# Six release blocks for the expert tiles where there were ten, with row tails cleared by plan and a new issue order

## Chip, core, metric

One core of a Trainium2 chip. The metric is the device time of one execution in microseconds; lower is better. The core's engines are PE (matrix multiply), DVE (vector), ACT (activation), POOL (here: indirect DMAs and small vector work) and SP (issues most DMAs).

## The reference, cut to what matters

```python
x = x + _L0_ffn(_L0_cond(x, dx, angle))        # bilinear warp of each 64x256 image, then a ternary-weight FFN (256-1024-256)
x = x + _L1_ffn(_L1_cond(x, ...))              # masked attention pooling, then 4 experts, each token goes to its top 2
x = x + _L2_ffn(_L2_cond(x, language_ids))     # adapter with layer norm, then a 256x256 frequency matrix
x = x + _L3_ffn(_L3_cond(x, cat_ids))          # per-image 256x256 matrix, then a ternary gate/up/down FFN
# in the experts:
h = gelu(einsum('nd,edh->enh', xf, w1) + b1)   # fp32, 256 -> 1024
y = einsum('enh,ehd->end', h, w2) + b2         # fp32, 1024 -> 256
out = einsum('nk,nkd->nd', gates, y_sel - c_sel + c_sum)   # of the two chosen experts
```

x has 128 images of 64 rows and 256 columns: 8192 tokens.

## The kernel before, in words

The images are worked in 32 groups of 4 (256 tokens, `QT`). Each engine runs a set of threads, written as Python generators: every `yield` ends a step, and `weave` (L214) strings the steps of all threads into one static instruction stream by a string of letters, `ORDER`, with one letter per step. Engines meet only at semaphores. So an engine that waits in one step holds up all that stands behind it in its string.

Per group there is a **front path**: POOL gathers windows of the image (`gather`, L1211), DVE does the warp (`warp`, L804 to L844), SP copies the result into row order (`regroup`, L624), then `front` (first FFN, L854 on DVE, L1489 on PE) and `attend` (pooling and router, L896, L1517). `attend` ends with a position for each of the 512 (token, expert) rows of the group; POOL writes the rows to their places in an arena in HBM (`scatter`, L1231), sorted by expert.

The groups are released to the experts in **blocks**, `BLOCKS` (L45): ten blocks of 2,2,3,4,4,4,4,4,3,2 groups. When the rows of a whole block are counted, `make_plan` (L982, DVE) writes which arena row and which expert each tile has. A block of n groups gets 2n full tiles of 256 rows and 3 half tiles of 128 (`NTILE`, `width`), since the four experts' shares do not end at tile borders. Per tile: SP loads its rows (L646) and 1 MB of the expert's first weights (L652), PE transposes (L1572), multiplies up (L1587) and down (L1603), ACT applies Gelu (L1389), DVE evicts (L1042), SP stores (L699). On PE the steps of two tiles overlap by one step.

When all tiles of a block are stored, `y_back` (POOL, L1245) gathers the rows of each of its groups back, and `back` (adapter and frequency matrix) and `last` (fourth layer, with the matmuls L1675, gate and up L1479, down L1485) finish the group. `back` and `last` have one set of buffers each and two of the image rows, so a group's `last` follows that of the group before.

The arena has two halves, used by blocks in turn. A tile may read rows that no token was written to, so the input arena is cleared first (L667), and the output arena too (L662): 17.8 MB of zeros from a row of zeros, at the head of SP's queue. The ternary weights of the two FFNs are made at the start from weights that SP loads one after another (L752); DVE's first reduction of each (L1162) waits for the load.

```python
NTILE = [2 * n * QT // TILE + EXP - 1 for n in BLOCKS]
pool.wait_ge(E["m_st"], 16 * TFIRST[BLOCK[q] + 1])    # y_back: all tiles of the block are stored
dve.wait_ge(E["run4"], BFIRST[b + 1])                 # make_plan: all groups of the block are counted
```

## Time and profile before

| | us |
|---|---|
| three runs | 2349.57, 2351.9, 2355.35; median 2351.9 |
| the profiled execution, span from first to last instruction | 2373.0 |
| first plan ready | 252.2 |
| first expert transposes on PE | 259.1 |
| last eviction of an expert tile ends | 2270.0 |

The profile's page gives busy times per engine and forty slices of the span, each digit a tenth of busy share. PEclk is the share of full clock that PE was granted. A row of the line groups ends with the idle time of the engine ahead of these instructions and what released it. Overlapping instructions of different lines are counted in each line's busy time, so the lines add up to more than the engine's own busy time.

### The profile page before, as it was taken

To read this page: it belongs to the slowest core of one execution; us is meant where nothing else is said; L and a number is where in the kernel's file an instruction comes from. 1 tells how busy PE (TensorE), PEld (TensorE's weight loads), DVE (VectorE), ACT (ScalarE), POOL (GpSimd) and SP (SyncE) were. 2 spreads that over 40 slices of the span, in tenths; PEclk is the share of its full clock that TensorE was granted. 3 is DMA by queue.
4 is the path that set the end of the run, shared out by engine and by line. 5 is a ranking of instruction groups with operands and counts; after the bars stand their busy time and mean duration, and the time that the engine had idled before them with its cause. 6 is when DMAs were issued, how large, how long until landed. Compare 5 with 4: busy or idle time off the path is not lost.

```text
span 2373.0 us, 47046 instructions
## 1 busy us (share of the span) xinstructions
PE 2056.5 (87%) x12000; PEld 1608.0 (68%) x12000; DVE 1769.0 (75%) x7891; ACT 1558.4 (66%) x2737; POOL 1029.2 (43%) x1092
## 2 busy tenths in 40 slices
PE   1065798999999999999999999999999999999965
PEld 1032577777777777777777777777777787778842
DVE  5589988878789888878988897789985454443444
ACT  1035566658686788768787878778875775765733
POOL 1356666645535564545446544456451212211120
PEclk8565799999999999999999999999999999999976
DMA  7833445454556455655556646456654555444521
GB/s 285 290 78 79 153 140 160 148 153 147 162 148 194 134 171 167 179 166 162 137 173 178 171 140 210 123 167 175 206 164 140 154 164 169 131 158 154 164 85 53
DMA packets 306118, 375.70 MB, mean 158 GB/s; under 512 B 127122, under 2 KB 251447, under 8 KB 292924
## 3 DMA queue, kind: packets, MB, share of 16 engines
q1 hardware_dynamic: 274848, 297.02, 41.7%
q0 software_dynamic: 28672, 68.21, 9.9%
q10 hardware_dynamic: 2332, 7.47, 0.8%
q8 instruction: 100, 1.64, 0.3%
q14 instruction: 166, 1.36, 0.2%
HBM read 291.23 MB, written 72.93 MB: 153 GB/s over the span
## 4 chain that ended last, share of the span: by engine, by line
PE 28%; DVE 11%; DMA 7%; SPq 7%; issue 5%; POOL 5%; ACT 1%; DVEq 1%; ACTq 0%; POOLq 0%
PE bank L1603 7%; PE bank L1587 7%; DMA w_win<-in_windows,w_idx 3%; PE bank L1479 3%; DVE w_prod L822 3%; POOL w_win L1211 2%; PE bank L1485 2%; PE bank L1657 2%; SPq L624 1%; PE bank L1467 1%; DMA moe_out_sorted<-moe_y 1%; DMA out<-x_back 1%; PE bank L1675 1%; DMA moe_y_back<-moe_out_sorted,rows_back 1%; PE bank L1473 1%
## 5 line engine op out<-in xcount | busy, mean ns | idle before, releaser
L1211 POOL DMA_INDIRECT w_win<-in_windows,w_idx x512 | 550.0, 1074 | 474.7 <-DMA w_win<-in_windows,w_idx 169.3
L1603 PE MATMUL bank<-moe_w,moe_hidden_T 128*128 x2528 | 634.4, 391 | 27.8 <-DVE moe_y L1042 19.2
L1587 PE MATMUL bank<-moe_xT,moe_w_tile 128*128 128x256 f32 (+1 forms) x3008 | 628.8, 353 | 4.0 <-ACT moe_xT L1372 3.9
L1587 PEld LDWEIGHTS bank<-moe_xT,moe_w_tile 128*128 128x128 f32 x3008 | 512.3, 194 | 74.9 <-issue 7.1
L1603 PEld LDWEIGHTS bank<-moe_w,moe_hidden_T 128*128 128x128 f32 x2528 | 469.8, 195 | 103.1 <-issue 42.6
L822 DVE TENSOR_TENSOR w_prod<-w_win,w_hat 128x36 f32<-128x36 f32 x4096 | 493.9, 216 | 6.8 <-issue 2.7
L1389 ACT ACTIVATE moe_hidden_T<-bank,moe_b 128x256 f32<-128x256 f32 (+1 forms) x752 | 288.4, 437 | 191.1 <-PE bank L1587 187.9
L1245 POOL DMA_INDIRECT moe_y_back<-moe_out_sorted,rows_back x128 | 127.7, 998 | 248.2 <-DVE rows_back L1052 116.4
L1231 POOL DMA_INDIRECT moe_in_sorted<-c,rows x128 | 139.2, 1088 | 150.4 <-issue 63.8
L1389 ACT ACT_TABLE_LOAD x128 | 164.2, 1283 | 56.2 <-PE bank L1587 54.6
L1129 DVE SCALAR_TENSOR_TENSOR hidden_back<-bank,back_stats,hidden_back 128x512 f32<-128x512 f32 x128 | 95.3, 744 | 110.8 <-ACT hidden_back L1429 110.2
L1429 ACT ACT_TABLE_LOAD x114 | 146.3, 1283 | 2.5
L879 DVE SCALAR_TENSOR_TENSOR hidden_front<-bank,front_stats,L_b_rows 128x512 f32<-128x512 f32 x128 | 95.2, 744 | 27.0 <-PE bank L1479 25.8
L1296 ACT ACTIVATE w_hat<-w_t 128x512 f32<-128x512 f32 x64 | 40.4, 631 | 113.4 <-DVE w_out L844 104.6
L1250 POOL TENSOR_SCALAR mean_var<-mean_var 128x2 f32<-128x2 f32 x32 | 14.3, 448 | 219.6 <-DVE mean_var L1082 219.0
L1429 ACT ACTIVATE hidden_back<-bank,back_stats 128x512 f32<-128x512 f32 x128 | 88.0, 688 | 31.6 <-PE bank L1479 30.1
L1479 PE MATMUL bank<-L_w_ternary,q1T_front 128*128 128x512 fp8e4 x256 | 84.4, 414 | 24.7 <-DVE hidden_front L879 21.9
L1042 DVE TENSOR_TENSOR moe_y<-bank,moe_offset_rows 128x512 f32<-128x512 f32 (+1 forms) x94 | 56.3, 599 | 63.0 <-PE bank L1603 38.0
L1479 PE MATMUL bank<-L_gate_ternary,q1T_back 128*128 128x512 fp8e4 x256 | 83.1, 409 | 23.2 <-DVE hidden_back L1129 20.9
L1359 ACT ACTIVATE q_front<-hidden_front,half_magic,front_tile_stats 128x1024 f16<-128x1024 f32 x64 | 79.3, 1239 | 28.5 <-DVE front_tile_stats L885 28.3
L1314 ACT ACTIVATE hidden_front<-hidden_front 128x1024 f32<-128x1024 f32 x64 | 67.7, 1058 | 44.4 <-DVE hidden_front L879 44.3
L1250 POOL TENSOR_SCALAR front_tile_stats<-front_tile_stats 128x1 f32<-128x1 f32 x64 | 16.8, 263 | 176.7 <-ACT q_front L1320 173.9
(258 smaller groups left out, 3803.0 us busy)
## 6 DMA issues: line engine op xcount, KB each, us to landing
moe_w_tile<-in_moe_w SPq DMA_DIRECT2D x94, 1024.0 KB
L_cond_W<-in_L_cond_W SPq DMA_DIRECT2D x128, 256.0 KB
adapters<-in_adapter SPq DMA_DIRECT2D x128, 192.5 KB
gamma_beta<-in_gamma_beta SPq DMA_DIRECT2D x128, 128.0 KB
moe_x<-moe_in_sorted SPq DMA_DIRECT2D x64, 256.0 KB
moe_out_sorted<-moe_y SPq DMA_DIRECT2D x64, 256.0 KB
x_front<-in_x SPq DMA_DIRECT2D x32, 256.0 KB
w_win<-in_windows,w_idx POOLq DMA_INDIRECT x512
```

Of the source, the lines that this page charges most:

```text
L822: ins = v.tensor_tensor(out3, win, hy, ALU.mult)
L879: v.scalar_tensor_tensor(HBA[:, n * 512:(n + 1) * 512], A0[:, :], sa[:, DQ][:, one(u)], b1B[:, n * 512:(n + 1) * 512], ALU.mult, ALU.add). ...
L1129: v.scalar_tensor_tensor(hb, B1[:, :], sbk[:, DQ][:, one(u)], hb, ALU.mult, ALU.mult).then_inc(E["b_hb"], 1)
L1211: gp.indirect_dma_start(out=V[:, g_ * WLEN:(g_ + 1) * WLEN], out_offset=None, in_=t["windows"], in_offset=bass.IndirectOffsetOnAxis(ap=idx ...
L1231: gp.indirect_dma_start(out=XS, out_offset=bass.IndirectOffsetOnAxis(ap=pos[par][:, c:c + 1], axis=0), in_=C1[:, u * D:(u + 1) * D], in_of ...
L1245: gp.indirect_dma_start(out=YG[:, c * D:(c + 1) * D], out_offset=None, in_=YS, in_offset=bass.IndirectOffsetOnAxis(ap=posb[:, c:c + 1], ax ...
L1359: return s.activation(to[:, :], hidden[:, :], ACT.Identity, bias=hmag[:, :], scale=scale)
L1389: ins = s.activation(hT[:, (f % (2 * FPU)) * TILE:(f % (2 * FPU)) * TILE + width(n)], (H0, H1)[r % 2][:, (f % FPU) * TILE:(f % FPU) * TILE ...
L1429: s.activation(HBB[:, n * 512:(n + 1) * 512], B0[:, :], ACT.Silu, scale=sbk[:, 6 * TT + u:6 * TT + u + 1]).then_inc(E["b_silu"], 1)
L1479: last = te.matmul(bank[:, :], q1t[:, d * QT + u * P:d * QT + (u + 1) * P], w[:, d * F + n * 512:d * F + (n + 1) * 512], start=(d == 0), s ...
L1587: last = te.matmul((H0, H1)[r % 2][:, (f % FPU) * TILE:(f % FPU) * TILE + width(n)], W1[n % 3][:, d * F + f * P:d * F + (f + 1) * P], XT[: ...
L1603: last = te.matmul(Y[:, u * D:(u + 1) * D], hT[:, (f % (2 * FPU)) * TILE + u * P:(f % (2 * FPU)) * TILE + (u + 1) * P], ap(moe2, weight + ...
```

## The change

`SUPERS` takes the place of `BLOCKS`: six blocks of 2, 4, 8, 8, 6 and 4 groups. `STRIDE` is 8, so no block is released in parts, and each has one plan of 2n + 3 tiles: 7, 11, 19, 19, 15 and 11, 82 where there were 94. The parts of `make_plan` for blocks released in several steps are in the code but never built.

Each expert's share of the arena gets 256 rows of slack. The input arena is no longer cleared at the start. When a block's plan is made, SP reads the four ends of the experts' rows from it and clears 256 rows behind each and 256 at the arena's end (`tails`); the block's first row load waits for these five writes. The output arena, larger now (18.9 MB in 20 writes), is cleared piece by piece behind the first groups (`zeros`), each piece after a given `a_x1`, the end of a group's front. Input and output arenas are two tensors each.

The four `ORDER` strings are new.

```diff
 TILE = 256
-BLOCKS = (2,2,3,4,4,4,4,4,3,2)
-NBK = len(BLOCKS)
-BFIRST = [sum(BLOCKS[:b]) for b in range(NBK + 1)]
-BLOCK = [b for b in range(NBK) for _ in range(BLOCKS[b])]
-NTILE = [2 * n * QT // TILE + EXP - 1 for n in BLOCKS]
+SUPERS = (2,4,8,8,6,4)
+STRIDE = 8
+HALVES = EXP - 1
+
+
+def steps():
+
+    out = []
+    for c, n in enumerate(SUPERS):
+        given = 0
+        for first in range(0, n, STRIDE):
+            groups = min(STRIDE, n - first)
+            final = first + groups == n
+            upto = 2 * n * QT // TILE + HALVES if final else 2 * (first + groups) * QT // TILE - (EXP - 1)
+            out.append((c, groups, upto - given, final))
+            given = upto
+    return out
...
+
+
+STEPS = steps()
+NSB, NBK = len(SUPERS), len(STEPS)
+SFIRST = [sum(SUPERS[:c]) for c in range(NSB + 1)]
+SUPER = [c for c in range(NSB) for _ in range(SUPERS[c])]
+BFIRST = [sum(g for _, g, _, _ in STEPS[:b]) for b in range(NBK + 1)]
+BLOCK = [b for b in range(NBK) for _ in range(STEPS[b][1])]
+NTILE = [n for _, _, n, _ in STEPS]
 TFIRST = [sum(NTILE[:b]) for b in range(NBK + 1)]
+STILE = [sum(n for k, _, n, _ in STEPS if k < c) for c in range(NSB + 1)]
 GT = TFIRST[NBK]
...
+def fresh():
+
+    out, seen = [], [0, 0]
+    for c, e in enumerate(ENDROW):
+        k = c % 2
+        new = [(c, k, r, min(ZSTEP, e + TILE - r)) for r in range(seen[k], e + TILE, ZSTEP)]
+        seen[k] = max(seen[k], e + TILE)
+        out += new
+    return out
+
+
+ZY = fresh()
+ZCOUNT = [sum(z[0] <= c for z in ZY) for c in range(NSB)]
 
 
...
 ORDER = {
     "vector":
-        "iciiciiiwiwiiwiwiwiwwiwiiwiwiwiwiwiwiwwwwiwiwiwiwwiwiwwiwiwiwiwiwwwwwwcwwwwifwfwfwiiffwiwifwfwwwfwffffwwfwwwfwwf"
...
+        "iiiciiiiiiwiwiwiwiwiiwwciwiwiwiwiiwwiiwiwiwiiwiwiwiwiwiwwwwwwwwwiwwwwiiwiwicfwffwfwwfwwfwfwwwfwffffwwfwwfwwfwfwf"
...
+                c, k, r, n = ZY[z]
+                sp.wait_ge(E["a_x1"], 2 * (max(SFIRST[c] - 2, 0) + (z - (ZCOUNT[c - 1] if c else 0)) // 3 + 1))
+                sp.dma_start(YS[k][r:r + n, :].rearrange("(p k) d -> p k d", p=P),
+                             ap(ZR, 0, [[0, n // P], [1, D]])).then_inc(E["z_y"], 16)
+
+            def tails(c):
+
+                yield
+                if c == 0:
+                    sp.wait_ge(E["z_set"], 1)
+                sp.wait_ge(E["plan"], BLOCK[SFIRST[c + 1] - 1] + 1)
+                if c > 1:
+                    sp.wait_ge(E["m_ld"], 16 * STILE[c - 1])
+                free = [sp.value_load(plan[0:1, PN_Z + EXP * c + e:PN_Z + EXP * c + e + 1], min_val=0, max_val=ENDROW[c])
+                        for e in range(EXP)]
+                for e in range(EXP):
+                    sp.dma_start(XS[c % 2][bass.ds(free[e], TILE), :].rearrange("(p k) d -> p k d", p=P),
+                                 ap(ZR, 0, [[0, TILE // P], [1, D]])).then_inc(E["zero"], 16)
+                end = ENDROW[c]
+                sp.dma_start(XS[c % 2][end:end + TILE, :].rearrange("(p k) d -> p k d", p=P),
+                             ap(ZR, 0, [[0, TILE // P], [1, D]])).then_inc(E["zero"], 16)
 
             def rows_in(n):
                 yield
...
                     for name in SCAT:
                         sp.wait_ge(E[name], 32 * BFIRST[TBLOCK[n] + 1])
+                    if STEPS[TBLOCK[n]][3]:
+                        sp.wait_ge(E["zero"], 16 * (EXP + 1) * (STEPS[TBLOCK[n]][0] + 1))
                 moe_rows(n)
...
                     yield
-                    if c == 0 and b < 4:
-                        pool.wait_ge(s_zero[b], 16 * len(pieces(ZX[b])))
                     if c == 0:
-                        if b > 1:
-                            pool.wait_ge(E["m_ld"], 16 * TFIRST[b - 1])
+                        if block > 1:
+                            pool.wait_ge(E["m_ld"], 16 * STILE[block - 1])
                         pool.wait_ge(E["a_pos"], q + 1)
                         pool.wait_ge(E["a_rc"], TT * (q + 1))
...
-                        pool.wait_ge(E["m_st"], 16 * TFIRST[BLOCK[q] + 1])
+                        pool.wait_ge(E["m_st"], 16 * STILE[SUPER[q] + 1])
```

Three places show how the strings move the work. First SP's queue at the start, where the zeros stand. Before:

```order
L667 DMA moe_in_sorted<-zero_row 1024x1x256 x2
L667 DMA moe_in_sorted<-zero_row 256x1x256
L667 DMA moe_in_sorted<-zero_row 1024x1x256 x2
L667 DMA moe_in_sorted<-zero_row 256x1x256
L662 DMA moe_out_sorted<-zero_row 1024x1x256 x4
L752 DMA raw<-in_L_gate 128x2048
L662 DMA moe_out_sorted<-zero_row 1024x1x256 x4
L662 DMA moe_out_sorted<-zero_row 512x1x256
L667 DMA moe_in_sorted<-zero_row 1024x1x256 x4
L752 DMA raw<-in_L_up 128x2048
```

With the change, at the same place:

```order
L630 DMA w_offsets<-w_offsets_all 1x128
L795 DMA raw<-in_L_gate 128x2048
L795 DMA raw<-in_L_up 128x2048
L620 DMA w_frac<-w_frac_all 128x2x16
L623 DMA w_shift_frac<-w_shift_frac_all 128x128 x2
L625 DMA w_idx<-w_idx_all 128x16
L795 DMA raw<-in_L_down 128x2048
L653 DMA c<-w_out 16x8x32 x12
```

The weight loads follow each other with no zeros between them; the zeros now stand among the regroup copies `c<-w_out`.

Second, PE at the border of two blocks. Before, ahead of the first tile of the third block:

```order
L1603 MATMUL bank<-moe_w,moe_hidden_T 128x256
L1473 MATMUL bank<-ident_f,q_front 128x128 x8
L1594 TENSOR_LOAD plan
L1603 ISA
L1603 MATMUL bank<-moe_w,moe_hidden_T 128x256
L1603 ISA
L1603 MATMUL bank<-moe_w,moe_hidden_T 128x256
L1572 MATMUL bank<-const,moe_x 128x128 x4
```

With the change, ahead of the first tile (L1637) of the third block, the first of eight groups:

```order
L1544 MATMUL bank<-L_gate_ternary,q1T_back 128x512 x2
L1544 MATMUL bank<-L_up_ternary,q1T_back 128x512 x2
L1626 MATMUL bank<-router_logits,const 128x8
L1627 MATMUL bank<-router_logits,ones 128x8
L1544 MATMUL bank<-L_gate_ternary,q1T_back 128x512 x2
L1544 MATMUL bank<-L_up_ternary,q1T_back 128x512 x2
L1544 MATMUL bank<-L_w_ternary,q1T_front 128x512 x2
L1538 MATMUL bank<-ident_f,q_front 128x128 x8
L1637 MATMUL bank<-const,moe_x 128x128 x4
```

Before, the first tile of each block from the second on follows the last tile of the block before at once. Now no expert matmul (L1652, L1668) stands in the 120 rows between the second block's last tile and this one; 3.7 groups' `front`, 3.9 `attend`, 3 `back` and 2.5 `last` do.

Third, PE behind the last expert matmul. Before:

```order
L1603 MATMUL bank<-moe_w,moe_hidden_T 128x256
L1473 MATMUL bank<-ident_f,q_back 128x128 x8
L1485 MATMUL bank<-L_down_ternary,q2T_back 128x256 x8
L1467 MATMUL bank<-const,x_back 128x128 x4
L1675 MATMUL bank<-L_cond_W,xT_last 64x256 x8
L1467 MATMUL bank<-ident_f,q_back 128x128 x4
```

With the change:

```order
L1668 MATMUL bank<-moe_w,moe_hidden_T 128x256
L1544 MATMUL bank<-L_gate_ternary,q1T_back 128x512 x2
L1544 MATMUL bank<-L_up_ternary,q1T_back 128x512 x2
L1532 MATMUL bank<-const,x_back 128x128 x4
L1544 MATMUL bank<-L_gate_ternary,q1T_back 128x512 x2
L1544 MATMUL bank<-L_up_ternary,q1T_back 128x512 x2
L1704 MATMUL bank<-xT_adapter,adapters 64x64 x8
```

Before, the group at work in `last` was group 28, at its down matmuls, and three L1675 (groups 29 to 31) were left. Now it is group 26, at its first gate matmul, and five of the same matmuls (L1740, groups 27 to 31) are left.

## Rows read from the trace of the kernel before

**Rows 1.** The page: span, busy times, two rows of the 40 slices.
```profile
span 2373.0 us, 47046 instructions
...
PE 2056.5 (87%) x12000; PEld 1608.0 (68%) x12000; DVE 1769.0 (75%) x7891; ACT 1558.4 (66%) x2737; POOL 1029.2 (43%) x1092
...
DVE  5589988878789888878988897789985454443444
...
GB/s 285 290 78 79 153 140 160 148 153 147 162 148 194 134 171 167 179 166 162 137 173 178 171 140 210 123 167 175 206 164 140 154 164 169 131 158 154 164 85 53
```

**Rows 2.** Table of stretches of the core, the columns named in its first line.
```profile
core 0: us, PE busy (x) PEld busy (x) DVE busy (x) ACT busy (x) POOL busy (x), PEclk, DMA share, GB/s
124.00:252.00 128.00, 73.51 (x278) 38.33 (x275) 114.26 (x622) 60.79 (x107) 82.48 (x82) 0.57 0.33 83
207.00:252.00 45.00, 26.57 (x90) 14.34 (x90) 39.34 (x223) 22.90 (x43) 32.47 (x33) 0.50 0.30 82
252.00:290.00 38.00, 30.92 (x151) 24.23 (x152) 35.65 (x199) 23.05 (x43) 20.52 (x25) 0.81 0.58 181
252.00:363.00 111.00, 100.26 (x529) 80.92 (x530) 101.16 (x547) 68.74 (x139) 63.93 (x71) 0.92 0.49 148
363.00:473.00 110.00, 99.71 (x560) 82.33 (x559) 95.67 (x533) 68.25 (x144) 74.67 (x74) 0.97 0.54 161
954.00:2270.00 1316.00, 1251.71 (x7525) 998.39 (x7523) 938.51 (x3962) 964.77 (x1644) 513.19 (x560) 0.97 0.54 162
2270.00:2373.00 103.00, 60.68 (x304) 33.63 (x304) 43.18 (x98) 31.18 (x44) 12.89 (x14) 0.67 0.26 78
```

**Rows 3.** Timeline of DVE, L844: start us, us, engine, line, operation, out<-in.
```profile
123.66 0.61 DVE L844 TENSOR_TENSOR w_out<-w_cols 128x256 f32<-128x256 f32 x1
...
241.73 0.61 DVE L844 TENSOR_TENSOR w_out<-w_cols 128x256 f32<-128x256 f32 x1
```

**Rows 4.** Groups by line and shape on PE: busy us, mean ns, idle before.
```profile
L1603 PE MATMUL bank<-moe_w,moe_hidden_T 128*128 x2528 | 634.4, 391 | 27.8 <-DVE moe_y L1042 19.2 <-ACT moe_hidden_T L1389 7.6 <-issue 0.3
L1587 PE MATMUL bank<-moe_xT,moe_w_tile 128*128 128x256 f32 x2048 | 496.1, 386 | 3.8 <-ACT moe_xT L1372 3.7
L1587 PE MATMUL bank<-moe_xT,moe_w_tile 128*128 128x128 f32 x960 | 132.8, 283 | 0.2 <-ACT moe_xT L1372 0.2
...
L1572 PE MATMUL bank<-const,moe_x 128*128 128x128 f32 x316 | 51.2, 278 | 1.5 <-DMA moe_x<-moe_in_sorted 1.5
```

**Rows 5.** Timeline of SP's queue near 60 to 90 us.
```profile
65.52 14.05 SPq L662 DMA_DIRECT2D moe_out_sorted<-zero_row  x5
...
89.62 2.62 SPq L752 DMA_DIRECT2D raw<-in_L_up  x1
```

**Rows 6.** Waits of DVE from 28 to 130 us: total us, times, longest.
```profile
DVE weight_sums L1162 <- DMA raw<-in_L_up: 15.3, 1, 15.3
DVE weight_sums L1162 <- DMA raw<-in_L_gate: 7.3, 1, 7.3
```

**Rows 7.** Timelines of DVE and PE around the first plan.
```profile
252.00 0.17 DVE L1026 TENSOR_TENSOR plan<-plan_work,const 128x21 int32<-128x21 f32 x1
...
259.11 1.06 PE L1572 MATMUL bank<-const,moe_x 128*128 128x128 f32 x4
```

**Rows 8.** The page, DMA issues: KB each, median us to landing.
```profile
moe_in_sorted<-zero_row SPq DMA_DIRECT2D x2, 256.0 KB, 7.7
```

**Rows 9.** The page, costliest groups: the eviction on DVE.
```profile
L1042 DVE TENSOR_TENSOR moe_y<-bank,moe_offset_rows 128x512 f32<-128x512 f32 (+1 forms) x94 | 56.3, 599 | 63.0 <-PE bank L1603 38.0
```

**Rows 10.** Timeline of PE behind the last expert tile.
```profile
2273.21 2.00 PE L1675 MATMUL bank<-L_cond_W,xT_last 128*64 128x256 f32 x16 [0.67 <-ACT xT_last L1417]
...
2279.19 1.03 PE L1479 MATMUL bank<-L_gate_ternary,q1T_back 128*128 128x512 fp8e4 x2 [0.69 <-ACT q1T_back L1363]
...
2309.38 2.00 PE L1675 MATMUL bank<-L_cond_W,xT_last 128*64 128x256 f32 x16 [0.68 <-ACT xT_last L1417]
...
2341.31 2.00 PE L1675 MATMUL bank<-L_cond_W,xT_last 128*64 128x256 f32 x16 [0.68 <-ACT xT_last L1417]
```

310 lines of the change are left out of this document (160 added, 150 removed).

## The prediction

> **What bounds the kernel now.** I read the page first. PE is busy 87% of the span and DVE 75%, but DVE's digits are high up to slice 30 and low behind it [rows 1]. The table of stretches then splits the run into three stages [rows 2]. From 954 to 2270 us PE works 1251.7 of 1316 us at a granted clock of 0.97: there PE sets the pace. From 124 to 252 us DVE works 114.3 of 128 us (89%) and PE 57%: there DVE does, through the warp. From 2270 us, the end of the last expert tile, to the end PE works 60.7 of 103 us and DVE 43.2: neither, but a chain of short steps through PE, ACT and DVE. The warps of the first and the fourth group end at 124.3 and 242.3 us [rows 3]: while DVE does little else, one group of the front path costs 39 us. So three things can move the end: the work on PE, the time at which PE is given tiles, and what is left when the tiles are done.
>
> **Sum, part by part.** The rows are of one execution of 2373.0 us span, 0.9% above the median of 2351.9; I add up in its time and scale by the ratio at the end.
>
> 1. *Fewer half tiles.* A block of n groups has 2n full and 3 half tiles: ten blocks give 64 and 30, six give 64 and 18. A half tile costs 132.8/30 = 4.4 us in L1587; L1603 did 2528 matmuls in 634.4 us, so its 16 take 4.0; two transposes 0.3: 8.8 us. A full one costs 496.1/64 = 7.8, 32 x 0.251 = 8.0 and 0.6: 16.4 us [rows 4]. Lines overlap: they add up to some 2336 us where PE is busy 2056.5, a factor of 0.88; and PE is busy 95% of the bound stretch. So 15.3 and 8.2 us of time. Twelve half tiles less are 98 us, if PE is the limit where they fall.
>
> 2. *The start.* Before, 17 MB of zeros stand on SP's queue ahead of two weight loads: from 65.5 us on nine of these writes are issued, and only at 89.6 us the load of the up weights [rows 5]. DVE waits 15.3 and 7.3 us for these loads [rows 6]. The new order issues both loads ahead of any zeros. Bounds 0 and 22.6 us; I take 18, since the wait is DVE's, and DVE bounds this stage. The first plan, ready at 252.2 us before [rows 7], now stands 4 us of DVE work later in its order: 238 us.
>
> 3. *Zeros later.* Twenty writes, eighteen of them of 1 MB, stand between the regroup copies of groups 1 to 15, seven of them in a row. Issue took 14.05 us for five [rows 5], so 2.8 each at most. A regroup copy behind seven could wait from 0 to 7 MB at the 285 GB/s of the first slice, 26 us [rows 1]; copies have a warp's time of slack, so I take 8. Here the shape of the queue matters. The Trainium skill, DMA: Bandwidth & Descriptors, section on queues, rings and completion order, says that SP has one row of rings whose descriptors are consumed in ring order; by that the copy waits for all seven and the sum would be 18 us higher. The load of the up weights, late behind zeros, agrees with it.
>
> 4. *The plan of the block of eight*, the third. This is the step on which most rests. DVE's work per group of the front path is 36 us (114.3 us [rows 2] for 3.2 warps, 3 fronts, 2.1 attentions). All of DVE is 1769.0 us [rows 1]: less 32 x 36, 56 us of evictions [rows 9] and 50 of preparation it leaves 16 us a group for back and last, 8 each. Up to the second plan DVE's order holds 4.1 groups of front path, 7 evictions and a plan: 155 us. Up to the third plan 7.9 groups (284 us), 5.0 backs and 3.9 lasts (70) and 11 evictions (10): 364 us. DVE's share in these stages is 0.89, 0.91 and 0.87, and 0.94 in the shortest stretch [rows 2]; I take 0.91. Second plan: 238 + 170 + 8 = 416 us. Third: 416 + 400 = 816. Before, groups came in blocks of 2, 2 and 3, each plan was in time, and PE was busy 91% from 252 to 473 us [rows 2]. Now PE has, between the last tile of block 1 and the first of block 2, 3.7 fronts, 3.9 attentions, 3 backs and 2.5 lasts, about 80 us of work; block 1 ends near 640 us. PE idles some 110 us.
> PE's clock matters there. From 207 to 252 us PE was 59% busy and was granted 0.50, its lower level of 1.2 GHz; from 363 to 473 us with 91% it had 0.97 [rows 2]. My sum needs no more PE time there, even at the lower level, as 80 us have 180 to lie in. But in that row DVE had only 87%. The Trainium skill, TensorE: Matmul & The Clock Gate, Part 1, says that an array that has been idle runs at 1.2 GHz; by that the steps for which DVE waits double in this stage, DVE stays at 0.87 and the sum is 18 us higher.
>
> 5. *Tails.* From plan to first transpose passed 7 us (252.2 to 259.1) [rows 7]. Now five zero writes of 256 KB wait for the plan, and the first tile for them: 7.7 us to land [rows 8] and 2 of issue. Hidden where PE has tiles left; exposed at the first three blocks, and it counts once, at the third, since the others lie ahead of a PE that waits anyway. First tile of block 2: 816 + 16 = 832 us.
>
> 6. *From there to the last tile.* PE still has 52 full and 12 half tiles, 16.3 fronts, 17 attentions and 22 backs and lasts. The stretch from 954 to 2270 us of before [rows 2] held 42 full and 18 half tiles and, within one group, the same of the others. So 1316 + 10 x 15.3 - 6 x 8.2, less 8 for the fewer lasts: 1412 us. The next block of eight needs DVE at 0.91 as well (about +10); behind it DVE is light (-10). The last tile ends at 832 + 1412 = 2244 us, 26 earlier than before.
>
> 7. *The end.* Before, when the last tile is done, PE's order holds three L1675, of groups 29 to 31, begun at 2273.2, 2309.4 and 2341.3; the run ends 31.7 us behind the last [rows 10]. Now it holds five, of 27 to 31, and group 26 is only at its first gate matmul; from there to the next L1675 it was 30 us (2279.2 to 2309.4 [rows 10]). So 28 + 4 x 32 + 32 = 188 us against 103: a block of four must be combined whole behind its last tile, and last has one set of buffers, so groups follow each other at 32 us.
>
> **Sum:** 2244 + 188 = 2432 us, 59 over 2373.0, or 2.5%. Times 2351.9/2373.0: **2410 us**. The last tile comes only 26 us earlier although half tiles and start give some 100: the wait for the third plan takes the rest. Then the end costs 85.
>
> **Rivals.**
> *DVE keeps pace (not slower).* Without back work to wait for and with PE free, DVE could run at 0.96. Then the plans come at 236 + 161 = 397 and 397 + 379 = 776 us, the first tile at 788; with 1390 us behind it and a tail of 175, 2353 us, or 2332 in the median's time. It decides at a third plan before about 770 us with such a tail. For it: 0.94 from 252 to 290 us [rows 2]. Against: that was 38 us long, and no longer stretch passes 0.91. Chance 0.20, also for mixtures that end level.
> *Zeros in the way.* The 18.9 MB take 66 us at 285 GB/s. If the writes hold the regroup copies at each of their clusters and DVE stalls for half of what I don't count, it is 30 us more: 2440 us. The waits for weight loads behind zeros [rows 6] speak for it; that the copies are issued a warp ahead of their use speaks against. The ring order that the Trainium skill gives in DMA: Bandwidth & Descriptors would be its mechanism. Chance 0.12.
> *The half tiles bring nothing.* If PE's wait in the bound stretch were for something else, the six fewer behind 832 us would save none of their 49 us: 2459 us. The 95% of PE speaks against it. Chance 0.08.
> *The forecast* has 0.60.
>
> **Range and chances.** A run of this kernel is told from no change by 0.3%. The forecast's own bounds (DVE share 0.87 to 0.94, zeros 0 to 26, start 0 to 22) are about 2365 to 2445. To hold 8 in 10 the range goes down into the first rival and up to the others: 2350 to 2455. Faster by over 0.3%: 0.17 from the first rival and 0.02 from the edge of the forecast, 0.19. Within: 0.07. Slower: 0.74.
>
> **What would show it.** Right: the third plan between 790 and 840 us, a gap of PE before it with a granted clock near 0.5; the first transposes of each block some 16 us behind its plan; PE's busy time near 1960 us; 180 to 195 us from the last eviction to the end with the matmuls that were L1675 some 32 us apart; no DVE wait for the gate and up weights. Wrong: PE busy over 90% from 600 to 800 us, or a last tile before 2200 us, or a tail under 150.

## The result and the profile after

The changed kernel takes 2462.5 us (median of four runs: 2458.52, 2460.67, 2464.4, 2477.05), the kernel before in the same set 2350.7: a ratio of 1.048 [1.045, 1.051]. It is slower, as forecast, and 7.5 us above the range (2350 to 2455). The profiled execution is that of 2464.4 us. The sum of the prediction stands in the time of the trace before, so it is set beside this one.

| us of the trace | before | forecast | after |
|---|---|---|---|
| first plan | 252 | 238 | 243 |
| second plan of the new blocks | - | 416 | 427 |
| third plan | - | 816 | 829 |
| first transposes of the third block | - | 832 | 852 |
| last eviction of an expert tile | 2270 | 2244 | 2272 |
| from there to the end | 103 | 188 | 190 |
| span | 2373 | 2432 | 2462.6 |

The page after, its parts 1 and 2, against [rows 1]:

```profile
span 2462.6 us, 45055 instructions
...
PE 2041.1 (83%) x11400; PEld 1554.0 (63%) x11400; DVE 1751.7 (71%) x7797; ACT 1473.1 (60%) x2582; POOL 1024.3 (42%) x1092
...
PE   1435797799966789999989998999998999998665
...
PEclk8655797899957799999999999999999999999676
```

PE has 600 matmuls fewer and yet only 15 us less busy time. Its digits show the two places where the forecast put the loss: a gap at slices 12 to 14 (about 680 to 860 us), where PEclk falls to 5, and the last three slices. By PE's timeline the second block's last down matmul ends at 676.5 us and the third block's first transposes begin at 852.2: 176 us without a tile, where the forecast had 192 (640 to 832).

The table of stretches after, to be held against [rows 2]:

```profile
124.00:243.00 119.00, 55.86 (x204) 30.13 (x204) 101.37 (x560) 55.73 (x99) 70.78 (x74) 0.50 0.51 147
243.00:427.00 184.00, 143.86 (x742) 109.12 (x743) 153.98 (x844) 104.91 (x210) 105.78 (x116) 0.82 0.56 159
427.00:829.00 402.00, 328.48 (x1778) 243.36 (x1777) 345.55 (x1725) 254.40 (x469) 230.78 (x248) 0.84 0.50 145
680.00:829.00 149.00, 98.77 (x489) 61.22 (x488) 124.26 (x591) 83.72 (x148) 85.76 (x97) 0.69 0.46 130
852.00:2272.00 1420.00, 1340.63 (x7874) 1075.08 (x7872) 954.28 (x4061) 967.49 (x1666) 536.81 (x578) 0.98 0.52 157
2272.00:2462.00 190.00, 118.81 (x605) 67.33 (x603) 88.23 (x196) 58.93 (x89) 28.19 (x31) 0.69 0.31 94
```

Up to the third plan DVE is the busier engine in every row (0.85, 0.84, 0.86, 0.83). From 680 to 829 us PE works 98.8 of 149 us; in the same place of the kernel before, 680 to 830 us, it worked 140.5 of 150 at a clock of 0.99. From 852 us PE is busy 94% of the time.

The groups of PE's matmuls after, against [rows 4]:

```profile
L1668 PE MATMUL bank<-moe_w,moe_hidden_T 128*128 x2336 | 572.1, 386 | 7.7 <-DVE moe_y L1108 5.5 <-ACT moe_hidden_T L1454 1.3 <-issue 0.6
L1652 PE MATMUL bank<-moe_xT,moe_w_tile 128*128 128x256 f32 x2048 | 504.1, 390 | 3.2 <-ACT moe_xT L1437 3.2
L1544 PE MATMUL bank<-L_w_ternary,q1T_front 128*128 128x512 fp8e4 x256 | 90.5, 441 | 36.9 <-DVE hidden_front L923 33.1 <-ACT q1T_front L1428 2.6 <-issue 1.2
L1550 PE MATMUL bank<-L_w_ternary,q2T_front 128*128 128x256 fp8e4 x512 | 81.8, 314 | 18.9 <-ACT q2T_front L1428 18.9
L1652 PE MATMUL bank<-moe_xT,moe_w_tile 128*128 128x128 f32 x576 | 79.1, 281 | 0.0
```

The half tiles' up matmuls fell from 132.8 to 79.1 us, the down matmuls from 634.4 to 572.1. The front's matmuls, untouched by the change, took 441 and 314 ns where the same groups before had means of 414 and 286. The growth lies ahead of the third plan, where the clock is low: 472 and 332 ns from 243 to 829 us against 402 and 273 before (252 to 829 us); behind it they took 380 and 283 (852 to 2272 us) against 391 and 273 (954 to 2270 us).

The third block, by the timelines of SP's queue and of PE. The plan was ready at 829.3 us:

```profile
831.90 2.87 SPq L705 DMA_DIRECT2D moe_in_sorted<-zero_row  x4
834.81 0.62 SPq L708 DMA_DIRECT2D moe_in_sorted<-zero_row  x1
836.31 0.38 SPq L682 DMA_DIRECT2D moe_w_tile<-in_moe_w  x1
839.45 0.34 SPq L777 DMA_DIRECT2D L_cond_W<-in_L_cond_W  x1
...
843.97 0.47 SPq L779 DMA_DIRECT2D L_cond_b<-in_L_cond_b  x1
845.35 0.40 SPq L676 DMA_DIRECT2D moe_x<-moe_in_sorted  x1
```
```profile
852.25 1.06 PE L1637 MATMUL bank<-const,moe_x 128*128 128x128 f32 x4
```

The five tail writes are issued by 835.4 us; then stand a weight load and eight loads for `last`, and the tile's own rows come only at 845.35 us.

The end, by the timeline of PE, against [rows 10]:

```profile
2300.44 2.00 PE L1740 MATMUL bank<-L_cond_W,xT_last 128*64 128x256 f32 x16 [0.68 <-ACT xT_last L1482]
2332.89 2.00 PE L1740 MATMUL bank<-L_cond_W,xT_last 128*64 128x256 f32 x16 [0.68 <-ACT xT_last L1482]
...
2431.65 2.00 PE L1740 MATMUL bank<-L_cond_W,xT_last 128*64 128x256 f32 x16 [0.68 <-ACT xT_last L1482]
```

Five of them from 2300.4 to 2431.7 us, 32.8 apart; the run ends 31 us behind the last.

### The profile page after: what moved, and what is told of

It is laid out like the page before. It is cut to its first block, busy times and chain, and to the rows that moved or that the text cites. A ratio compares the mean times of both kernels' runs of the same rounds, so it can differ in the third digit from the quotient of the medians.

```text
span 2462.6 us, 45055 instructions
## 1 busy us (share of the span) xinstructions
PE 2041.1 (83%) x11400; PEld 1554.0 (63%) x11400; DVE 1751.7 (71%) x7797; ACT 1473.1 (60%) x2582; POOL 1024.3 (42%) x1092
## 4 chain that ended last, share of the span: by engine, by line
PE 27%; SPq 9%; DVE 6%; DMA 5%; issue 4%; POOL 3%; ACT 2%; DVEq 0%; ACTq 0%; POOLq 0%
PE bank L1652 7%; PE bank L1668 6%; PE bank L1544 3%; SPq L653 2%; PE bank L1550 2%; DMA adapters<-in_adapter 2%; PE bank L1722 2%; PE bank L1532 1%; PE bank L1704 1%; DMA out<-x_back 1%; PE bank L1740 1%; PE bank L1538 1%; POOL w_win L1278 1%; SPq L764 1%; DVE w_prod L866 1%
## 5 line engine op out<-in xcount | busy, mean ns | idle before, releaser
L1652 PE MATMUL bank<-moe_xT,moe_w_tile 128*128 128x256 f32 (+1 forms) x2624 | 583.2, 366 | 3.2 <-ACT moe_xT L1437 3.2
L1668 PE MATMUL bank<-moe_w,moe_hidden_T 128*128 x2336 | 572.1, 386 | 7.7 <-DVE moe_y L1108 5.5
L1652 PEld LDWEIGHTS bank<-moe_xT,moe_w_tile 128*128 128x128 f32 x2624 | 463.5, 195 | 71.7 <-issue 8.7
L1668 PEld LDWEIGHTS bank<-moe_w,moe_hidden_T 128*128 128x128 f32 x2336 | 430.3, 192 | 76.1 <-issue 21.9
L1454 ACT ACTIVATE moe_hidden_T<-bank,moe_b 128x256 f32<-128x256 f32 (+1 forms) x656 | 258.8, 447 | 234.5 <-PE bank L1652 231.5
L1544 PE MATMUL bank<-L_w_ternary,q1T_front 128*128 128x512 fp8e4 x256 | 90.5, 441 | 36.9 <-DVE hidden_front L923 33.1
L1544 PE MATMUL bank<-L_gate_ternary,q1T_back 128*128 128x512 fp8e4 x256 | 88.6, 433 | 34.2 <-DVE hidden_back L1195 30.0
L923 DVE SCALAR_TENSOR_TENSOR hidden_front<-bank,front_stats,L_b_rows 128x512 f32<-128x512 f32 x128 | 95.2, 744 | 11.1 <-PE bank L1544 7.7
L1428 ACT ACTIVATE q2T_front<-bank 128x1024 bf16<-128x1024 f16 x64 | 65.4, 1022 | 55.2 <-PE bank L1538 55.1
L1550 PE MATMUL bank<-L_w_ternary,q2T_front 128*128 128x256 fp8e4 x512 | 81.8, 314 | 18.9 <-ACT q2T_front L1428 18.9
L1428 ACT ACTIVATE q2T_back<-bank 128x1024 bf16<-128x1024 f16 x64 | 65.5, 1023 | 52.6 <-PE bank L1538 52.5
L1210 DVE SCALAR_TENSOR_TENSOR x_back<-bank,back_tile_stats,x_back 128x256 f32<-128x256 f32 x64 | 30.8, 481 | 89.4 <-PE bank L1550 86.0
```

The source lines that it names most:

```text
L1428: return s.activation(to, bank, ACT.Copy, bias=-HMAGIC, scale=1.0)
L1454: ins = s.activation(hT[:, (f % (2 * FPU)) * TILE:(f % (2 * FPU)) * TILE + width(n)], (H0, H1)[r % 2][:, (f % FPU) * TILE:(f % FPU) * TILE ...
L1544: last = te.matmul(bank[:, :], q1t[:, d * QT + u * P:d * QT + (u + 1) * P], w[:, d * F + n * 512:d * F + (n + 1) * 512], start=(d == 0), s ...
L1550: last = te.matmul(bank[:, 0:D], q2t[:, f * P:(f + 1) * P], w[:, f * D:(f + 1) * D], start=(f == 0), stop=(f == NFB - 1))
L1652: last = te.matmul((H0, H1)[r % 2][:, (f % FPU) * TILE:(f % FPU) * TILE + width(n)], W1[n % 3][:, d * F + f * P:d * F + (f + 1) * P], XT[: ...
L1668: last = te.matmul(Y[:, u * D:(u + 1) * D], hT[:, (f % (2 * FPU)) * TILE + u * P:(f % (2 * FPU)) * TILE + (u + 1) * P], ap(moe2, weight + ...
```

## Experiments

Each set ran on a chip of its own. The kernel before took 2516 us on that of set A, 2509 on B, 2359 on C, 2354 on D and 2366 on E. Each ratio is to the kernel before in its own set. Across sets, C, D and E are compared with each other and with the first result; A and B are compared with each other alone.

**A. Taking the change apart.** Four kernels. The change rewrote all five `ORDER` strings, POOL's too. `e1_old_blocks`: the code after with the ten blocks and the orders of before; zeros of the output behind the first groups, tails by plan.

```diff
-SUPERS = (2,4,8,8,6,4)
+SUPERS = (2,2,3,4,4,4,4,4,3,2)
```


> The changed kernel with the ten blocks and the order of the kernel before (2, 2, 3, 4, 4, 4, 4, 4, 3, 2): weight loads first, tails cleared behind each plan, output arena cleared late in 12 writes, but neither large blocks nor the new order. Theory A (the cost lies in the blocks and the order; the clearing is hidden, the start gains 18 us): about 2335 us, 0.7% under before. Theory B (the writes of zeros hold the regroup copies or the first tiles, wherever the blocks end): 2365 us or more, over before. The first plan tells too: near 235 us by A, 250 or later by B.

`e2_tails_late`: after, with the wait for the tails moved from a block's first row load to its first tile that can hold a tail, and SP's step for the tails (`t` in its string) placed behind the step that loads the block's first rows (`l`).

```diff
-                    if STEPS[TBLOCK[n]][3]:
-                        sp.wait_ge(E["zero"], 16 * (EXP + 1) * (STEPS[TBLOCK[n]][0] + 1))
+                if TFIRST[TBLOCK[n] + 1] - n == 2 * HALVES:
+                    sp.wait_ge(E["zero"], 16 * (EXP + 1) * (STEPS[TBLOCK[n]][0] + 1))
```


> The changed kernel, but only the first tile that can be partly empty waits for the cleared tails, and the clearing is issued behind the first tile's load. If the zero writes are what holds the first tile of each block (theory: step 5), the first transposes of the third block come 8 to 12 us behind the plan instead of 23, and the run is 8 to 12 us shorter, near 2452 us. If it is the eight loads for last that stand in SP's queue between plan and tile load, it stays at 18 us or more and the time within 4 us of the changed kernel's 2462.

`e3_loads_first`: before, with the two weight loads ahead of the nine zero steps in SP's order. `e4_zeros_first`: after, with all twenty output zeros behind those loads and no wait for `a_x1`.

```diff
-    "gxxmgzzzzizzzzzigi...
+    "gxxmgiizzzzzzzzzgi...
```
```diff
-                sp.wait_ge(E["a_x1"], 2 * (max(SFIRST[c] - 2, 0) + (z - (ZCOUNT[c - 1] if c else 0)) // 3 + 1))
```


> The kernel before, with only the two late raw weight loads moved ahead of the nine groups of zero writes in SP's order. By step 2 of the forecast DVE's waits of 15.3 and 7.3 us go, the first plan comes 18 us earlier (234 us) and the run ends up to 18 us earlier: 2335 us. Rival: the writes of zeros fill the queues all the same and the regroup copies or window gathers wait in their place: first plan not before 248 us, time within 5 us of 2351.

> The changed kernel with its twenty zero writes of the output arena in a row behind the two weight loads, none of them waiting for a front. If the late writes between regroup copies cost what my step 3 left out (theory: 10 to 25 us by the second and third plan), the second plan comes before 415 us, the third before 810 and the time falls to about 2445. Rival: 18.9 MB ahead of the first regroup copies hold DVE's first warps for 30 us or more, the first plan comes after 265 us and the time rises to 2480 or more.

Measured: e1 1.003 [0.999, 1.007]; e2 1.021 [1.013, 1.028]; e3 1.006 [1.002, 1.010]; e4 1.033 [1.026, 1.041]. With the old blocks and orders the rest of the change costs nothing that this chip shows. e2 left 21 us from third plan to first transposes, so the wait for the tails wasn't what held the tile: with tails out of the way SP issued a weight load at 859.8 us, its next load only at 866.5, and then the same eight loads. e3 shows that the 22.6 us of [rows 6] can't be had by moving the loads: its first plan came at 264 us, and the wait had moved on to the third load. DVE's waits in e3, 40 to 270 us:

```profile
DVE weight_sums L1170 <- DMA raw<-in_L_down: 37.2, 1, 37.2
```

e4 has its first three plans at 284, 470 and 902 us. The change itself, on the chip of B, had them at 248, 435 and 868, and e2, on e4's own chip, at 246, 430 and 859: all twenty writes at the head of SP's queue make the plans 34 to 37 us later than where the change has them, 38 to 44 against e2.

**B. Order and border.** `e5_changed_again`: the change on this chip. `e6_new_order`: the same blocks, its five orders written anew by one rule that I also used for the next two. `e7_split_plan`: e6 with the block of eight (groups 6 to 13) given to the tiles in two plans. `e8_short_end`: e6 with a last block of 2 and 2.

```diff
-        for first in range(0, n, STRIDE):
-            groups = min(STRIDE, n - first)
+        stride = (2, 4, 4, 8, 6, 4)[c]
+        for first in range(0, n, stride):
+            groups = min(stride, n - first)
```
```diff
-SUPERS = (2,4,8,8,6,4)
+SUPERS = (2,4,8,8,6,2,2)
```


> The changed kernel itself, on the chip of this set of runs, as the measure for the runs beside it. The first set ran on a chip where the kernel before took 2516 us instead of 2351. If the loss is in the program alone the ratio to before is again 1.045 to 1.05; if a part of it was the chip's, it is another, near the 1.02 of the run with the tails late.

> The changed kernel with all of its blocks, tails and zeros, but another order on each engine: an expert tile's parts on PE stand behind any other work that could run at that moment, on ACT and DVE ahead of it, and last and back stand close behind the block that frees them. Theory A (what my forecast rests on: DVE's work ahead of the third plan and the four groups behind the last tile are a matter of the blocks): within 15 us of the changed kernel. Theory B (the order costs as much as the blocks: the front path waits for others in it): third plan 30 us or more earlier than in the changed kernel and a time 30 to 60 us under it.

> As the run with the new order, and ordered by the same rules, but the first block of eight (groups 6 to 13) is released in two plans, after four groups and after eight: five full tiles come with the first. If PE's wait for the plan of eight costs what step 4 says, these five tiles (15 us each of PE) fill PE's gap between the second block's last tile and the fourth plan, and the time is 25 to 60 us under the run with the new order. Rival: PE is not what is short later on, the gap closes with waits elsewhere, and the difference is under 10 us.

> As the run with the new order, but the last block of four groups is two blocks of two: three more half tiles. By step 7 the end behind the last tile falls from 190 us or so to 105 to 130. By step 1 the three half tiles cost 25 us. So the sum would be 20 to 50 us under the run with the new order. Rival: the last tile comes later by as much as the end gets shorter, since PE's work of the last groups lies ahead of it instead of behind: within 10 us.

Measured: e5 1.024 [1.018, 1.030], so this chip shows half the loss of the first; e6 1.061 [1.054, 1.067]: my rule's order is itself 3 to 4% worse, and e7 and e8 are read against e6 alone. e7 1.045 [1.039, 1.051]: 35 us less than e6 by the medians, 40 by the ratios. e6 had no tiles from 752 to 856 us, 104 us; in e7 the next ones start at 753, right behind block 1. So a closed gap gave back a third to two fifths of its length, in this order; the change's own gap of 176 us was not closed in its own order. e8 1.054 [1.048, 1.059]: the end after the last tile is 57 us shorter (114.2 for 171.6), but the last tile comes 60 us later, of which three more half tiles are some 25 by the forecast's first step; over the runs 12 to 18 us are gained, with intervals that overlap, in the two profiled runs none. A gain is not shown.

**C. Sizes by doubling.** `e9_zeros_double`: each late zero write is issued twice, the second to a spare arena, and the stores of tiles wait for both. `e10_three_loads_first`: before, with three weight loads ahead of the zeros. `e11_pe_filler`: after, with two idle transposes ahead of each PE step between block 1's last tile and block 2's first. `e12_ten_by_rule`: e6's rule with ten blocks.

```diff
                 sp.dma_start(YS[k][r:r + n, :].rearrange("(p k) d -> p k d", p=P),
                              ap(ZR, 0, [[0, n // P], [1, D]])).then_inc(E["z_y"], 16)
+                sp.dma_start(YD[k][r:r + n, :].rearrange("(p k) d -> p k d", p=P),
+                             ap(ZR, 0, [[0, n // P], [1, D]])).then_inc(E["z_y"], 16)
```
```diff
+        tiles += name == "e"
+        if eng == "tensor" and tiles == 9 * TFIRST[2] and name != "e":
+            filler()
```


> The changed kernel with each of the twenty late zero writes issued twice, the second time into a spare arena. In the changed kernel's trace DVE's loads of the window addresses take 1.8 to 1.9 us instead of 0.6 while such writes run (20 slow loads, 25 us in excess, 19 of them before 800 us). Theory Z (these writes cost DVE's path what my steps 3 and 4 missed, 13 us by the third plan and more): with twice the writes the slow loads double, the third plan comes 13 to 25 us later than the changed kernel's and the end as much. Rival (the slow loads lie in waits that DVE has anyway): slow loads double but the plans and the end move by less than 6 us.

> The kernel before with all three late raw weight loads, the down weights too, ahead of its nine groups of zero writes; nothing else. In the run with two of them moved, DVE waited 37 us for the third behind the zeros and the first plan came at 264 us. Theory: now DVE waits under 10 us for weights, the first plan comes 15 to 25 us before the 264 of that run, and since PE bounds this kernel from 252 us on, the run ends 10 to 20 us before the kernel before, ratio 0.992 to 0.996. Rival: the zeros then meet the first regroup copies and window gathers and take back what the loads gave: ratio 1.0.

> The changed kernel with two transposes of the identity into an idle bank ahead of each of PE's 106 steps between the last tile of the second block and the first of the third: work that nothing needs. In that stretch PE was 71% busy and granted 0.75 (640 to 829 us, with the tail of the second block in it). Theory C (PE's lower clock there holds the DVE steps that wait for it): the granted clock of the gap rises to 0.95, DVE waits less for PE and the third plan comes 5 to 15 us earlier, measured from the second plan. Rival: DVE's own work sets the pace and the filler only delays it: third plan 0 to 10 us later.

> The changed kernel's code with the ten blocks of before, but ordered by the same rules as the run with the new order. That run (six blocks) stood at 1.061 of before, where the changed kernel stood at 1.024. If blocks and order add up, the ten blocks under these rules stand at 1.061 less what the six blocks cost, 0.020 to 0.025: 1.036 to 1.041. If large blocks cost nothing and the changed kernel's order was its whole loss: 1.055 or more.

Measured: e9 1.063 [1.061, 1.065]; plans at 264, 457 and 864 us against 243, 427 and 829; last eviction and end 27 us later; 35 us more by the ratios (to e16, below). Twenty more writes cost some 30 us; the ten of them ahead of the first plan cost 21 there. DVE's waits for the regroup copies up to the first plan, in the change (124 to 243 us) and in e9 (124 to 264 us):

```profile
DVE front_stats L904 <- DMA c<-w_out: 1.9, 1, 1.9
```
```profile
DVE front_stats L907 <- DMA c<-w_out: 11.8, 2, 10.7
```

So doubling made a wait of 10 us that the change itself does not have. The rest of what it added is in DVE's own register loads, each slow while zeros are written (last section). Above their usual time they took 11 us up to the first plan, 8 more up to the second and 5 more up to the third in the change, 22, 17 and 10 in e9. The added 11, 9 and 5, with the copies' 10 at the first plan, are the 21, 9 and 5 us by which the plans came later, stage by stage.

e10 1.000 [0.999, 1.002]: the wait moved once more, to the regroup copy behind the zeros. DVE's waits in e10, 40 to 260 us:

```profile
DVE front_stats L868 <- DMA c<-w_out: 34.5, 2, 34.2
...
DVE weight_sums L1170 <- DMA raw<-in_L_down: 1.6, 1, 1.6
```

SP's queue in e10, behind six zero writes begun at 78.0 us:

```profile
91.86 24.37 SPq L670 DMA_DIRECT2D moe_out_sorted<-zero_row  x9
116.27 9.31 SPq L675 DMA_DIRECT2D moe_in_sorted<-zero_row  x4
125.62 12.30 SPq L632 DMA_DIRECT2D c<-w_out  x16
```

SP issued zeros until 125.6 us and the copies only then, until 137.9; DVE went on at 139.2. So the copies were late because SP was still issuing the writes ahead of them.

e11 1.040 [1.037, 1.043]. The stretch of e11 and, under it, that of after (PE's columns only):

```profile
680.00:830.00 150.00, 104.22 (x709) 0.89 0.47 136
```
```profile
680.00:830.00 150.00, 99.77 (x495) 0.69 0.46 130
```

The clock rose. The third plan came 396 us behind the second, where the change had 402 in the first result and 399 in e16, and the span stayed (2458.3 against 2458.9 of e16). The ratio is 0.007 under e16's, across two chips. So the clock is worth 0 to 17 us, and I can't say which. e12 1.113 [1.109, 1.117] tells only that my rule writes poor orders; it separates nothing.

**D. Who issues the zeros.** `e13_before_zeros_act`: before, its zeros issued by ACT on its own queue behind its third step of the initial work (`init`). `e14_zeros_act`: the same for after, all twenty, and the first store of a tile waits for all of them. `e15_old_blocks_zeros_act`: e1 with its twelve zeros issued in e13's place, with the same wait. `e16_changed_fast_chip`: the change. The edit of e14, the `zeros` thread taken off SP and given to ACT:

```diff
-                if n == STILE[c]:
-                    sp.wait_ge(E["z_y"], 16 * ZCOUNT[c])
+                if n == 0:
+                    sp.wait_ge(E["z_y"], 16 * len(ZY))
...
-                  out_mid=each(x_out, q_), zeros=each(zeros, range(len(ZY))),
+                  out_mid=each(x_out, q_), 
...
+                act.dma_start(YS[k][r:r + n, :].rearrange("(p k) d -> p k d", p=P),
+                              ap(ZR, 0, [[0, n // P], [1, D]])).then_inc(E["z_y"], 16)
```


> The kernel before with its nine groups of zero writes issued by ACT, which is idle from 46 to 104 us, on ACT's own queue, instead of by SP. With the writes on SP's queue DVE waited 22.6 us for the weights behind them, and with the weights ahead of them 34 us for a regroup copy behind them (first plan 252 and 258 us). Theory Q (it is the place in SP's queue): both waits go, the first plan comes at 230 to 240 us and the run is 8 to 18 us shorter, ratio 0.992 to 0.997. Rival B (it is the bandwidth: 17 MB take their 50 us from whatever runs beside them): first plan at 250 or later, ratio 1.000 within 0.002.

> The changed kernel with its twenty zero writes issued by ACT at the start, on ACT's own queue, and the first store of a tile waiting for all of them. The run with each late write doubled was 0.0146 of before slower than the changed kernel (1.0625 against 1.0479), its third plan 35 us later. If a write costs as much the first time as the second and the early ones on ACT's queue cost little: third plan near 800 us instead of 829 and a ratio of 1.033 to 1.040. Rival: 18.9 MB at the start cost as much as late: ratio 1.045 or more.

> The changed kernel's code with the blocks and order of before (1.003 of before in the first set) and its twelve zero writes issued by ACT at the start. It writes 10.8 MB of zeros at the start instead of 17.4, and 12.5 MB of tails behind the ten plans. Theory: the start gains 20 us and more on before; what is left of it at the end shows the price of the tails in the stage that PE bounds: ratio 0.990 if they are hidden, as step 5 says of blocks that find PE busy, 1.000 or more if each of the ten plans' five writes costs 2 to 4 us.

> The changed kernel once more, on the chip of this set, as the measure for the run with its zeros on ACT's queue. 1.048 of before if this chip is like the one of the forecast, 1.024 if like that of the first two sets.

Measured: e13 **0.994** [0.992, 0.997], first plan at 238 us, 2340.2 us: faster than both kernels. e14 1.054 [1.050, 1.058], first plan at 273 us. ACT's timeline in e14, then in e13:

```profile
41.93 58.93 ACTq L1547 DMA_DIRECT2D moe_out_sorted<-zero_row  x20
100.91 0.63 ACT L1383 ACTIVATE w_hat<-w_t 128x512 f32<-128x512 f32 x1 [58.40 <-issue]
```
```profile
53.28 28.48 ACTq L1485 DMA_DIRECT2D moe_out_sorted<-zero_row  x9
81.79 15.97 ACTq L1490 DMA_DIRECT2D moe_in_sorted<-zero_row  x4
97.86 0.63 ACT L1319 ACTIVATE w_hat<-w_t 128x512 f32<-128x512 f32 x1 [53.09 <-issue]
```

ACT stands still for the issue of the writes in both, some 3 us each. What differs is who waits for it: in e13 ACT had done two rounds of `w_hat` (the weights that DVE's `w_prod` multiplies with) ahead of the writes, and no wait of DVE from 28 to 240 us is over 5.8 us; in e14 it had done one, and DVE waits:

```profile
DVE w_t L847 <- issue: 35.3, 1, 35.3
```

The view names no releaser, but DVE's `w_t` begins at 103.3 us, as ACT's next round of `w_hat`, which reads the same tile, ends. So e14 was late by my placing of the writes; whether their number would have cost too, a run with the twenty behind the second round would tell, and there is none. From its first plan to the third it took 572 us, where the change took 586 and 582: without writes in that stretch 10 to 14 us come back. That is what its slow register loads took there (13 us over the usual in the change, 15 in e16, 1 in e14). The regroup copies held DVE as long as in the change, 10.5 us here (450 to 845 us) and 9.9 there (427 to 829 us):

```profile
DVE front_stats L926 <- DMA c<-w_out: 10.5, 2, 5.6
```
```profile
DVE front_stats L904 <- DMA c<-w_out: 9.9, 3, 5.9
```

e15 1.013 [1.010, 1.016] and e16 1.048 [1.044, 1.051]. From e13 to e15 the tails, with the slack and the two tensors that belong to them, cost 44 us in ten blocks; from e15 to e16 blocks, orders and late zeros cost 82. DVE's waits over the whole run in e15, then in e13:

```profile
DVE moe_y L1216 <- DMA moe_out_sorted<-moe_y: 42.9, 6, 11.8
```
```profile
DVE moe_y L1065 <- DMA moe_out_sorted<-moe_y: 20.5, 6, 5.3
```

**E. Tails by themselves.** `e17_tails_double`: after, five more tail writes per plan, to a spare arena, waited for too. `e18_old_tails_late`: e15 with the tails treated as in e2.

```diff
+                for e in range(EXP + 1):
+                    sp.dma_start(XD[TILE * (EXP * c + c + e):TILE * (EXP * c + c + e + 1), :].rearrange("(p k) d -> p k d", p=P),
+                                 ap(ZR, 0, [[0, TILE // P], [1, D]])).then_inc(E["zero"], 16)
...
-                        sp.wait_ge(E["zero"], 16 * (EXP + 1) * (STEPS[TBLOCK[n]][0] + 1))
+                        sp.wait_ge(E["zero"], 32 * (EXP + 1) * (STEPS[TBLOCK[n]][0] + 1))
```


> The changed kernel with the five tail writes behind each final plan followed by five more into a spare arena, for which the first tile waits as well. With the blocks of before the tails stood for 1.0129 against 0.9943 with the input arenas cleared at the start: 44 us over ten plans, 4.4 us a plan. If the second five cost as much as the first, six plans give 26 us: ratio 1.0476 + 0.011 = 1.059, the first transposes of each of the first four blocks 4 to 5 us later behind their plan. Rival (step 5 of the forecast: only the third block's counts, the others are hidden): under 9 us, ratio 1.048 to 1.051.

> The run with the blocks of before and the zeros on ACT's queue (1.0129), but the five tail writes of each block are issued behind the block's first tile and weight loads, and only the first tile that can be partly empty waits for them. In that run PE waited 17.5 us for tile loads and DVE 42.9 us for stores of tiles, against 20.5 us for stores where there are no tails. If the cost is the wait of the first tile for the writes: ratio 1.000 to 1.005. If it is the writes' place on SP's queue ahead of loads and stores, whoever waits: the waits move but the ratio stays at 1.009 or more.

Measured: e17 1.052 [1.050, 1.055], 11 us over e16 with intervals that overlap. By doubling, the tails of six plans cost some 10 us in the changed kernel, which is not clear of noise. e18 1.007 [1.004, 1.009], 15 us better than e15; 29 us against e13 stay, and DVE still waits 45.7 us for the stores of the tiles where e13 has 20.5.

## Why the prediction was right and where it failed

The direction held, and so did the two places of the loss: a plan for eight groups that comes too late, and an end four groups long. The sum was 30 us short in the trace's time.

- *Fewer half tiles*, -98: right. L1668 fell by 62.3 us, the half tiles' L1652 by 53.7 and the transposes by 3.5, 119.5 in all and 105 times 0.88. But PE's busy time was 2041 us, not near 1960. The step counted matmuls and not their speed: all groups of PE add up to 2298 us after and 2336 before, only 39 less, since the others grew by some 80 (the front's two are above). The front's grew where DVE is the busier engine, so this is hardly a loss of its own; that is argued.
- *The start*, -18 to a first plan at 238: 243 measured. The two waits of [rows 6] did go, but the third load kept DVE 7.4 us, and nine slow register loads took 11. e3, e4 and e10 show that the zeros at the head of SP's queue are paid by whatever is behind them; e13, with ACT issuing them, takes both waits out.
- *Zeros later*, +8: **the step that failed**, in its size and in what it priced. It priced the regroup copies alone. Their slack held: they kept DVE 1.9 us up to the first plan, nothing up to the second, and 9.9 up to the third, no more than in e14, which writes no zeros there. What the step put at nothing is that DVE's own register loads get slow while zeros are written: nineteen of them took 24 us over the usual up to the third plan. So the term is 24 us in this trace and 26 in e16's, where the forecast had 8; e14, with 10 to 14 us back between first and third plan, and the parts of e9 bear it out. e9's plain doubling (21, 30 and 35 us at the three plans, 27 at the end) also holds a wait of 10 us that one set of writes does not make. The rival *Zeros in the way* (+30, chance 0.12) comes nearer in size: 16 to 18 us more than the forecast were measured. That is luck, as its mechanism, held regroup copies, is not in the changed kernel. Ring order (the Trainium skill, DMA: Bandwidth & Descriptors, queues, rings and completion order) would have made 26 of the 8, near the size too and for the same wrong reason: behind the seven writes DVE waited 1.9 us. Nor do e10's copy, 34.2 us late, and the up weights of the kernel before, issued at 89.6 us, show it: SP issued them only when it was done with the writes.
- *The plan of the block of eight*: second plan to third took 402 us, forecast 400. Two errors cancelled: DVE worked 346 us there, not 364, and was busy 0.86, not 0.91. The +18 that the prediction set against it for the clock (the Trainium skill, TensorE: Matmul & The Clock Gate, Part 1) put DVE at 0.87, which is near what came; but with the clock raised from 0.84 to 0.91 over this stretch in e11 DVE rose to 351.2 of 402 us, 0.87, where e16 has 349.2, and 3 to 6 us came back. So the clock explains a part at most. The rival *DVE keeps pace* is out: a third plan at 829 us, not before 770.
- *Tails*, 16 us from plan to transposes: 22, 28, 23 and 23 in the first four blocks. The size was off by 7 and the cause was another: not the landing of the writes but the nine other loads that SP issues between tails and row load (the timeline above, and e2, which left 21). In ten blocks tails cost more than the first tile's wait: e18 takes that out and 29 us stay. DVE's longer waits for the tiles' stores point there; it isn't shown.
- *From there to the last tile*, 1412 us: 1420. The saving of the half tiles came, so the rival *The half tiles bring nothing* (1461 us by its terms) is out. New is a wait of PE in this stretch, from 852 to 2272 us after, and from 954 to 2270 us before:

```profile
PE bank L1704 <- DMA adapters<-in_adapter: 26.0, 14, 4.7
```
```profile
PE bank L1639 <- DMA adapters<-in_adapter: 7.5, 3, 3.1
```

These are 18.5 us more, while other waits of PE fell (for `moe_y` from 10.1 to 1.4, for `c_adapter` from 18.0 to 11.9). In all PE was idle 79 of 1420 us against 64 of 1316 before, some 10 more for the length. This would cover the 8; that the adapters are what was lost is argued, not tried.
- *The end*, 188 us: 190. Five matmuls 32.8 us apart. What I had not asked is whether a shorter end is a gain: e8 took 57 us off it and the last tile came 60 later.

By the milestones the 30 us are 5 at the first plan, 6 more at the second, 2 more at the third, 7 at the tile behind it, 8 in the stretch and 2 at the end. The 16 to 18 us of the late zeros more than cover the 13 at the plans; the other terms up to there were 3 to 5 too large. In the median's time 2410 + 30 is 2440, inside the range. **The other 22 us are in no step but in the scaling** by 2351.9/2373.0: the trace of before ran 0.9% over its median, the trace of after at its own (2464.4 against 2462.5). I took the ratio as exact. Later profiled runs stand up to 0.7% from their medians on either side (e9 16 us below, e12 19 above), which belonged into the range.

Open: how the 82 us from e15 to e16 divide. The late zeros are some 25 of it. Gap and end would be the rest, but neither was removed without a new order, and my orders were worse than the one of the change; what the change's own order costs beside its blocks was not separated either. The gap's 35 to 40 us and the end's 12 to 18 were measured in those. Open too is why the chip of B shows 1.024 for the change where those of the first result and of D show 1.048, and why e1 is level with before on A's chip though e15, which pays no zeros on SP, is 1.013 on D's.

## What to carry to other kernels

When a transfer is moved off the head of a queue, price it by what stands behind it in its new place and by what else slows while it runs. Double it there once, and read which waits grew, since the doubled kernel can wait for something that the single one does not wait for. The zeros cost at either place on SP's queue, and in the kernel before 14 us came back when an engine issued them for which nobody waited (e13). A release for a whole large block saves part tiles and pays twice, in the wait for its plan and in what is left behind its last tile; closing the first gave back less than its length, and shortening the second gave nothing clear of noise, since work only moves. Sum in one trace's time, but let the range carry how far that trace stands from its median.

## What the runs showed of the hardware

DVE loads a register with a window's offset ahead of each group of eight `w_prod`. This took 0.6 us in general, but up to 2.0 us while zeros were being written. The register loads of after over the whole run (least, median and greatest ns), and DVE's timeline behind the three writes issued at 142.7 us:

```profile
L837 DVEq TENSOR_LOAD <-w_offsets x512: 591/597/2034, 44.8 to 1632.6; - x171
```
```profile
144.50 0.95 DVE L866 TENSOR_TENSOR w_prod<-w_win,w_hat 128x36 f32<-128x36 f32 x8
146.35 0.97 DVE L866 TENSOR_TENSOR w_prod<-w_win,w_hat 128x36 f32<-128x36 f32 x8 [0.90 <-issue]
148.49 0.97 DVE L866 TENSOR_TENSOR w_prod<-w_win,w_hat 128x36 f32<-128x36 f32 x8 [1.17 <-issue]
```

Twenty such loads took over 1.2 us in after, 25 us above the usual in all, forty-one in e9 with 52 us, twelve in before. Nineteen of after's twenty lie ahead of the third plan: nine ahead of the first (11.1 us), six ahead of the second (7.7), four ahead of the third (5.1). In e9 these are 17, 13 and 8 (22.1, 16.8 and 10.1 us). So most of what late zeros cost is a load that waits behind no queue of its own; why it does is open.

The issue of a DMA held the issuing engine: SP issued nineteen writes for 47.6 us (e10), ACT stood still for 53.1 us with nineteen (e13) and for 58.4 us with twenty (e14), and the first two of e13 took only 0.62 and 0.69 us. In the kernel before ACT stood idle ahead of the same instruction for 58.9 us anyway, so in e13 nobody waited for it.
